# Flamingo gated cross-attention block: two more tiles of x turned by DMA as 16-bit planes

## The reference

```python
x = x + tanh(g_xattn[0]) * xattn(layernorm(x), ctx_768, mask, Wq, Wk, Wv, Wo)
x = x + tanh(g_ffn[0]) * ffn(layernorm(x), clip_x, clip_down, w_gate, w_up, w_down)

def xattn(x, context, mask, Wq, Wk, Wv, Wo):
    q, k, v = x @ Wq, context @ Wk, context @ Wv          # split into 16 heads
    attn = softmax(where(mask, q k^T * 32 ** -0.5, max_neg))
    return (attn @ v) @ Wo

def ffn(x, clip_x, clip_down, w_gate, w_up, w_down):      # fq: fake quantisation to 8 bits
    gate, up = fq(x) @ fq(w_gate).T, fq(x) @ fq(w_up).T
    return fq(silu(gate) * up) @ fq(w_down).T
```

## Time and profile before

| | us |
|---|---|
| median of 3 runs | 622.02 |
| lowest, highest | 621.38, 625.34 |
| the profiled execution | 622.02, its span 620.2 |
| TensorE busy | 599.1 (97%) |
| VectorE busy | 516.2 (83%) |
| ScalarE busy | 376.2 (61%) |
| GpSimd busy | 235.0 (38%) |

### The profile page before, as it was taken

One profiled execution on the slowest core, in us unless ns is written; L12 is line 12 of the kernel. 1 busy time (PEld: TensorE's weight loads), 2 busy tenths in 40 slices (PEclk: granted clock), 3 DMA queues, 4 the chain that ended last, 5 costly groups with the idle time before them and its releaser, 6 DMA issues. The chain is left out here.

```text
span 620.2 us, 12091 instructions
## 1 busy us (share of the span) xinstructions
PE 599.1 (97%) x3706; PEld 447.3 (72%) x3727; DVE 516.2 (83%) x957; ACT 376.2 (61%) x484; POOL 235.0 (38%) x473
## 2 busy tenths in 40 slices
PE   8999999999999999999999986999999999899997
PEld 6789899999999999999999873444444444444544
DVE  6786989999999998999899757888888888866765
ACT  5554677777777777777675534555555553355653
POOL 6251454454544454535433113111111110067775
PEclk9999999999999999999999997999999999999999
DMA  8539745454444445535643000386554110099633
GB/s 304 180 98 259 182 82 100 92 86 102 91 89 94 96 85 106 112 71 116 131 89 72 16 0 2 81 244 227 200 132 127 34 26 10 9 373 417 252 117 121
DMA packets 118459, 77.89 MB, mean 126 GB/s; under 512 B 98163, under 2 KB 100621, under 8 KB 118413
## 3 DMA queue, kind: packets, MB, share of 16 engines
q1 hardware_dynamic: 113169, 60.51, 38.6%
q10 hardware_dynamic: 5244, 16.82, 7.8%
HBM read 32.48 MB, written 21.36 MB: 87 GB/s over the span
## 5 line engine op out<-in xcount | busy, mean ns | idle before, releaser
L1447 ACT ACTIVATE sb_silu<-ps_g,sb_sgu 128x512 f32<-128x512 f32 x88 | 60.5, 687 | 72.1 <-PE ps_g L1542 43.8
L1542 PE MATMUL ps_g<-sb_xqT,sb_wgu 128*128 128x512 bf16 x344 | 89.2, 379 | 1.0 <-DVE sb_xqT L1498 0.6
L1542 PE MATMUL ps_u<-sb_xqT,sb_wgu 128*128 128x512 bf16 x346 | 89.4, 379 | 0.3
L1513 DVE SCALAR_TENSOR_TENSOR sb_h<-ps_u,sb_sgu,sb_silu 128x512 f32<-128x512 f32 (+1 forms) x88 | 66.1, 751 | 19.9 <-PE ps_u L1542 19.6
L1064 PE MATMUL ps_q<-sb_xT_hi,sb_wq_hi 128*128 128x256 f32 x256 | 75.3, 294 | 0.7 <-DVE sb_q_lo L769 0.6
L632 ACT ACTIVATE sb_prob<-sb_prob 128x616 f32<-128x616 f32 x64 | 45.6, 713 | 48.9 <-DVE sb_prob L795 48.9
L1623 POOL TENSOR_TENSOR sb_wgu<-sb_wgu,sb_x 128x512 f32<-128x512 f32 x31 | 53.5, 1727 | 52.2 <-DVE sb_wgu L1680 51.2
L1066 PE MATMUL ps_q<-sb_xT_hi,sb_wq_lo 128*128 128x256 f32 x256 | 72.4, 283 | 0.0
L1065 PE MATMUL ps_q<-sb_xT_lo,sb_wq_hi 128*128 128x256 f32 x256 | 72.3, 283 | 0.0
L1747 PE MATMUL ps_z<-sb_wdT,sb_hq 128*128 128x512 bf16 x324 | 71.2, 379 | 0.3
L1517 DVE TENSOR_REDUCE sb_hmax<-sb_h 128x1 f32<-128x512 f32 (+1 forms) x88 | 60.4, 686 | 7.6
(11 more groups left out here) (238 smaller groups left out, 1422.4 us busy)
## 6 DMA issues: line engine op xcount, KB each, us to landing
h_spill<-sb_h SPq DMA_DIRECT2D x4, 2816.0 KB, 9.1
sb_h<-h_spill ACTq DMA_DIRECT2D x16, 704.0 KB, 6.8
out_dram<-sb_wgu SPq DMA_DIRECT2D x31, 256.0 KB, 2.3
sb_x<-in_x_dram ACTq DMA_DIRECT2D x1, 4096.0 KB, 21.5
sb_w_in<-in_L_ffn_w_gate_dram SPq DMA_DIRECT2D x11, 256.0 KB, 2.7
sb_w_in<-in_L_ffn_w_up_dram SPq DMA_DIRECT2D x11, 256.0 KB, 2.6
sb_x<-in_x_dram SPq DMA_DIRECT2D x2, 1024.0 KB, 14.2
sb_x<-in_x_dram SPq DMA_DIRECT2D x2, 512.0 KB, 4.8
```

Of the source, the lines that this page charges most:

```text
L1447: act.activation(silu[(j * KI + i) % 2][:, :, :].rearrange("p t n -> p (t n)"), p_g[(j * KI + i) % 2][:, :], ACT.Silu, scale=sgu[:, i:i + ...
L1513: dve.scalar_tensor_tensor(steps_h, p_u[(j * KI + i) % 2][:, :, :], sgu[:, KI + i:KI + i + 1], silu[(j * KI + i) % 2][:, :, :], ALU.mult, ...
L1542: last = pe.matmul(banks[(j * KI + i) % 2][:, :], wgu[:, what, k, i * P:(i + 1) * P], xqT[j][:, k, :], start=(k == 0), stop=(k == KD - 1))
```

## The change

```diff
-DIRECT = 8
+DIRECT = 6
```

## The result

The changed kernel is slower. Its median is 632.25 us (631.51 to 633.56, 4 runs) beside 621.81 us for the kernel before on the same chip (621.38 to 625.34, 4 runs), 10.4 us or 1.7% more. The ratio estimated from all these runs, which is not the quotient of the two medians, is 1.0142, 95% interval 1.0113 to 1.0171; on 621.81 us that is 7.0 to 10.6 us. The profiled executions are 631.51 and 622.02 us, their spans 629.7 and 620.2: 9.5 us apart. The 0.9 us between 9.5 and 10.4 are spread between executions and not a place in the trace.

A forecast was written before the change was run, and what follows sets the result against it. TensorE, busy 97% of the span, was taken to bound the kernel. Wait 8.3, less transposes 0.36 and idle 1.14, plus clock 2.35, gave +9.1 us on 622.0: 631.1 us, range 626 to 636.5.

The forecast's parts named there:

- case A: Slot 2: ScalarE's join of tile 6 waits for planes held up by the load of x; 628.5 to 634 us, chance 0.62.
- TensorE sets the pace from slot 4 on, and nothing gives time back: Attention stage: slots of 10.58 us, TensorE busy throughout, so a shift of slot 4's start moves the kernel's end equally.
- Landing of the planes: Tile 6's planes, behind weight block 1's transpose on SP's queue, land at 61.5 us; bounds 60.6 and 67.2.
- Issue on SP: SP issues tile 6's planes at 49.0 us, taking 1.2 to 2.1 us, ahead of weight rows 3 at 51.88.
- ScalarE's chain of 3.9 us and TensorE's resumption: After the landing, ScalarE's join through copy of probabilities takes 3.9 us; TensorE resumes at 65.4, not 57.11: +8.3 us.
- The four transposes of slot 3: Tile 7's four TensorE transposes in slot 3 go away, giving back 0.36 us.
- the idle before L1146: Slot 4: TensorE's wait before the output transposes, caused by late weight rows 3, disappears: -1.14 us.
- The clock: TensorE's 8.6 us idle halves its clock until 4.7 us after resumption, costing +2.35 us.
- Tile 7 hidden: Tile 7's planes, ready near 65.7, land at 68.8 us, before ScalarE's join near 71: 2 us to spare.
- B: Same wait for tile 6, smaller: clock costs nothing (628.8 us) or shorter standstill, planes near 58 (627.6); chance 0.16.
- C: Tile 6's planes meet a second DMA standstill of 4.4 us under the load: +13.5, 635.5 us; chance 0.12.
- D: Tile 6's transfer is hidden, landing by 52.1 us (decisive: before about 53.2); 0.7 us won, 621.3 us; chance 0.10.

## Why the prediction was right, point by point

The forecast was 631.1 us, the result 632.25; the mechanism is case A's, and it was tested by taking the load away (621.63) and by moving it (the loss moved to tile 7).

**TensorE sets the pace from slot 4 on, and nothing gives time back.** Right: 9.09 us at slot 4's queries, 9.30 at 387.17, 9.5 at the end.

**Landing of the planes: 61.5 predicted, 61.1 measured.** The time is right, and so is the way to it: the transpose of block 1 landed at 59.2 (59.3 predicted), the planes 1.9 us behind it (2.2 predicted). The working is rough in one place: the load had only 33 packets left after 59.3, not 150. The rate of 817 packets a microsecond for what goes alone did most of the last piece, and that was a row. The landing also varies: 12.4, 13.1, 14.0 and 14.2 us after the issue in the four profiles with the planes in this place (the last two with the added matmuls).

**Issue on SP: 1.2 to 2.1 us predicted, 4.64 measured.** Wrong. With it weight rows 3 were issued at 53.41 and not 51.88. The prediction had said that such a slip costs nothing; that was right, VectorE's L931 waited for nothing after.

**ScalarE's chain of 3.9 us and TensorE's resumption: +8.3 predicted, +7.90 measured** (65.01 for 57.11). The chain took 65.01 - 61.1 = 3.9; the 0.4 are the landing's.

**The four transposes of slot 3, -0.36, and the idle before L1146, -1.14.** Both right: L1064 follows L1130 with no transposes between them, and the transposes at L1146 show no wait.

**The clock: +2.35 predicted.** Mis-sized. Without its 1.14 and 0.36 us, the stretch from L1119 to slot 4's queries in the earlier trace rows is 68.43 - 57.11 - 1.50 = 9.82 us; it took 12.51, so +2.7 (+2.9 against the kernel with TensorE kept busy). Half clock lasted 6.2 us after the resumption and not the 4.7 of the earlier trace rows; in the second profile 4.2. The sum then is 7.90 - 0.36 - 1.14 + 2.69 = 9.09. It has to come out, as the 2.69 are what the other terms leave. That it meets the 9.1 predicted so closely is luck: the errors of +0.4 and -0.35 cancelled. As a forecast of the parts it was good to half a microsecond, not to a hundredth.

**Tile 7 hidden.** Right: planes issued 65.41, landed 3.4 us later at 68.8; the join came at 73.16 (71 predicted), without a wait. Two steps on the way were off. The prediction's 65.7 isn't 61.5 + 2.8; with the split of 1.04 us these give 65.3, and the planes were issued at 65.41. And ScalarE came to the join 12.0 us after the first landing and not 9.6, since it waited 4.41 us for query matmuls that ran at half clock.

**The rivals.** B had two ways. The clock costs nothing: excluded by 2.0 to 2.9 us measured. The standstill gone: with the copies moved, the planes did land near 58 as B has it, but that took an edit, and no execution of the changed kernel shows it. C, a second standstill, is not seen; the landings of 13.1 and more are short of the +4.4 us it needs. D is what the kernels with the load in parts or in halves show, and its point of decision (landing before 53.2) is consistent with 52.7 and no wait of TensorE's.

How the planes' landing follows what lies beside them (tile 6's, issued at 48.1 to 48.7 in all but the second, at 44.8 there; the last row is tile 7's, issued at 60.0):

| load beside the planes | load landed at | planes landed at |
|---|---|---|
| 4 MB, six copies ahead (the change) | 60.4 | 61.1 |
| 4 MB, copies behind | 57.5 | 57.7 |
| 2 MB | 51.4 | 52.7 |
| 1 MB | 47.8 | 51.5 |
| 4 MB, a slot later | 72.6 | 73.1 |

In every profile in which the load outlasts the 3.1 us that the planes need alone, they land 0.2 to 1.5 us behind it.

**Open.** What makes the standstill between 51.5 and 56. With the load a slot later, six copies, a transpose and the planes follow each other on SP's queue as before, with the load issued beside them, and nothing stands still (248 GB/s or more in every microsecond from 57 to 70); so copies ahead of a transpose are not enough to make one. Why the transpose issued at 41.84 with the copies moved sent its first packets only near 46.5. Why TensorE's matmuls are slow from 7.6 to 16.6 us in the profiles of the kernel before with the load in parts and in halves.

## What to carry to other kernels

A DMA that takes over work from an engine is to be priced by what runs on the DMA engines, and what stands ahead of it on its queue, at the moment of its issue: the same 256 KB landed after 3.1 us or after 12.4 here, and the median over the 24 such transfers of the kernel before showed only the first. An engine that works in order and waits for that DMA holds up everything behind it, so count the queue behind the wait, and then what the idle time does to TensorE's clock. If a bulk load is the cause, move or cut the load: that took back the whole loss, though against the kernel before it won 0.2% at most.

## What the runs showed of the hardware

- Small packets beside a bulk load from another queue go one for one: 160 packets of 256 B and 162 of 2 KB in one microsecond with the copies later, 234 and 236 in the standstill of the kernel before from 51.5 to 56. So a transpose gets an eighth of the bytes that the load gets (0.04 and 0.33 MB).
- The issue itself takes longer beside a load: for the planes 1.23 to 1.31 us in a free place, 2.64 and 2.88 beside 2 MB of load, 2.86 to 5.51 beside 4 MB. What stands behind it on the queue is issued later: weight rows 3 at 53.41 for 51.88.
- TensorE's clock fell after far shorter idling than the prediction had in mind, and not every time. At the end of the attention stage TensorE idles 1.79 us before L1119, in the kernel before (at 359.31) as in the one with 50 added matmuls. In the first the clock stayed at 1.00, in the second it went to half. First the kernel before, then the other:

```profile
359.31 0.74 PE L1119 MATMUL ps_p<-sb_identf,sb_prob 128*128 128x128 f32 x5 [1.79 <-DVE sb_o_sb L808]
```

```profile
359.00:360.00 1.00, 0.69 (x7) 0.72 (x8) 0.16 (x1) 0.34 (x1) 0.00 (x0) 1.00 0.00 0
```

```profile
368.95 1.24 PE L1119 MATMUL ps_p<-sb_identf,sb_prob 128*128 128x128 f32 x5 [1.79 <-DVE sb_o_sb L808]
```

```profile
369.00:370.00 1.00, 1.00 (x6) 1.00 (x7) 0.00 (x0) 0.00 (x0) 0.00 (x0) 0.52 0.00 0
```

  The batch takes 1.24 us for 0.74. Whether the spread of one to two microseconds between executions comes from this in part is not shown.
- How long half clock lasts after TensorE resumes isn't one number: 3.4 us with 36 matmuls added, 4.2 and 6.2 in the two profiles of the changed kernel, 4.8 with the load a slot later, 7.6 with the copies later.
